# Weighting of one token group moved between engine slots, and two residual adds moved from VectorE to GpSimd, at the end of a recurrent layer with a routed MLP

## The reference, cut to what matters

```python
x2  = layernorm(x)
s   = sigmoid(x2 @ gate_w.T)                       # 32 experts
ids = top_k(s + e_bias, 4); w = s[ids] / sum(s[ids])
y   = sum over the 4 chosen experts of w * ((silu(x2 @ w1[e]) * (x2 @ w3[e])) @ w2[e])
out = x + layernorm(y)
```

## Time and profile before

| | us |
|---|---|
| median of three runs | 341.08 |
| the three runs | 341.17, 339.55, 341.08 |
| the profiled execution, whole | 339.52 |
| its span, first to last instruction | 337.7 |
| busy in the span: PE, DVE, POOL, ACT | 272.0, 250.5, 235.1, 215.6 |
| mean granted TensorE clock | 0.894 of full |

### The profile page before, as it was taken

How to read it: one execution, slowest core, us unless ns; L and a number is a source line. 1 busy time by engine, 2 the same in 40 slices (tenths; PEclk the granted TensorE clock), 3 DMA queues, 4 the chain that set the end, 5 groups by cost and what they waited for, 6 DMA issues and landing times.

```text
span 337.7 us, 6535 instructions
## 1 busy us (share of the span) xinstructions
PE 272.0 (81%) x1489; PEld 218.4 (65%) x1490; DVE 250.5 (74%) x952; ACT 215.6 (64%) x562; POOL 235.1 (70%) x273
## 2 busy tenths in 40 slices
PE   4664586654763989999999999998999999899930
PEld 2243253433642879889887889997967667799810
DVE  3778787887797487697446979863567897698796
ACT  6928867989633545556554556655458858875782
POOL 4396777776777777777763777777777777777700
PEclk9976767978555899999999999999999999999965
DMA  4999999961113455677745899977532111251232
GB/s 103 320 304 287 280 279 287 314 164 48 56 47 94 136 176 175 184 206 208 211 139 161 204 260 267 260 211 211 140 90 54 48 50 51 56 149 47 57 93 63
DMA packets 83999, 54.81 MB, mean 162 GB/s; under 512 B 8032, under 2 KB 80512, under 8 KB 83968
## 3 DMA queue, kind: packets, MB, share of 16 engines
q1 hardware_dynamic: 57472, 30.85, 33.6%
q0 software_dynamic: 6912, 14.17, 14.9%
q10 hardware_dynamic: 19584, 9.44, 9.9%
HBM read 25.07 MB, written 29.36 MB: 161 GB/s over the span
## 4 chain that ended last, share of the span: by engine, by line
PE 61%; DVE 14%; ACT 10%; issue 6%; POOL 6%; DMA 2%; SPq 0%; ACTq 0%; DVEq 0%
PE bank L1758 13%; PE bank L1794 9%; PE bank L1838 6%; PE bank L1826 6%; POOL xs_dram L438 6%; PE bank L1829 5%; PE bank L1775 5%; PE bank L1753 5%; PE bank L1587 4%; PE bank L1628 1%; PE bank L1580 1%; ACT hn L484 1%; ACT xnT L556 1%; DMA wi_raw<-in_L_attn_Wi_dram 1%; DVE left L825 1%
## 5 line engine op out<-in xcount | busy, mean ns | idle before, releaser
L438 POOL DMA_INDIRECT xs_dram<-xn_all,row_xs x108 | 108.3, 1002 | 37.0 <-issue 32.3
L447 POOL DMA_INDIRECT yk<-ys_dram,row_ys x108 | 106.0, 982 | 38.8 <-issue 26.9
L1758 PE MATMUL bank<-w,xbT 128*128 x288 | 59.8, 331 | 0.0
L693 ACT COPY xbT<-bank 128x256 f32<-128x256 f32 x72 | 26.9, 373 | 30.6 <-PE bank L1753 28.8
L1794 PE MATMUL bank<-w2s,aT 96*128 x288 | 45.8, 281 | 0.1
L1758 PEld LDWEIGHTS bank<-w,xbT 128*128 128x128 f32 x288 | 45.6, 192 | 0.2
L1203 DVE TENSOR_TENSOR act_a<-silu,bank 128x192 f32<-128x192 f32 x72 | 25.3, 351 | 26.4 <-ACT silu L696 25.9
L1794 PEld LDWEIGHTS bank<-w2s,aT 96*128 96x128 f32 x288 | 37.7, 191 | 2.0 <-issue 1.3
L696 ACT ACTIVATE silu<-bank 128x192 f32<-128x192 f32 x72 | 23.8, 331 | 18.9 <-PE bank L1758 17.2
L1212 DVE COPY yb<-bank 128x256 f32<-128x256 f32 x72 | 30.3, 421 | 7.3 <-PE bank L1794 5.5
L1838 PE MATMUL bank<-at_at,xn_all 128*128 128x256 f32 (+1 forms) x88 | 31.2, 437 | 3.7 <-DVE at_at L1472 3.7
(11 more groups left out here) (234 smaller groups left out, 526.9 us busy)
## 6 DMA issues: line engine op xcount, KB each, us to landing
xb<-xs_dram SPq DMA_DIRECT2D x144, 64.0 KB
ys_dram<-yb ACTq DMA_DIRECT2D x72, 128.0 KB
xs_dram<-zeros SPq DMA_DIRECT2D x2, 2048.0 KB, 15.0
ys_dram<-zeros SPq DMA_DIRECT2D x1, 2816.0 KB, 13.5
ys_dram<-zeros SPq DMA_DIRECT2D x1, 2560.0 KB, 18.1
x_sb<-in_L_attn_x_dram SPq DMA_DIRECT2D x8, 256.0 KB, 5.4
xs_dram<-xn_all,row_xs POOLq DMA_INDIRECT x108, 4.4
yk<-ys_dram,row_ys POOLq DMA_INDIRECT x108, 2.5
```

Source lines behind the costliest of these rows:

```text
L438: pool.indirect_dma_start(out=xs[h], out_offset=bass.IndirectOffsetOnAxis(ap=row_xs[:, j, k:k + 1], axis=0), in_=xn2_all[:, j, :], in_offs ...
L447: pool.indirect_dma_start(out=yk[h][:, j - h * TP, k, :], out_offset=None, in_=ys[h], in_offset=bass.IndirectOffsetOnAxis(ap=row_ys[:, j, ...
L1758: ins = pe.matmul(ps_gu[o][:, b * 2 * I:(b + 1) * 2 * I].rearrange("t (w a i) -> t w a i", w=2, a=1), xbT[:, o, b, :], w13[:, :, bass.ds(e ...
```

## The change

Five edits, in ACT's, DVE's, POOL's and SP's programs:

1. ACT weights its two tiles of group 6 behind the silus of pieces 41 and 42 instead of behind the loop, and the roots for groups 4 and 5 and the first dense tiles go from behind piece 42 to behind piece 43.
2. DVE does the first three steps of `weigh_in_6` behind piece 43 and the fourth behind piece 45 (before: one behind each of 45, 46 and 47, and the fourth behind the loop).
3. DVE does both `inverse_last` behind piece 44, `norm_d(0)` behind 46, `add_d(0)` behind 47, and the first sum over group 6's ACT-weighted rows also behind 47.
4. The adds of groups 4 and 5 leave DVE; POOL does them behind its last gather, each as one TENSOR_TENSOR of 128x512, waiting for the normed rows (`a_last`) and counting `p_xn`.
5. SP's waits follow: for groups 4 and 5 on `p_xn`, for the rest on a `c_fin` that doesn't count these two.

```diff
+        BY_POOL = [4, 5]
...
             for n, g in enumerate(ORDER):
-                sp.wait_ge(c_fin, n + 1)
+                if g in BY_POOL:
+                    sp.wait_ge(p_xn, 6 + BY_POOL.index(g))
+                else:
+                    sp.wait_ge(c_fin, sum(m not in BY_POOL for m in ORDER[:n + 1]))
...
+            for g in BY_POOL:
+                at = slice(g * GT, g * GT + routed(g))
+                pool.wait_ge(a_last, g + 1)
+                pool.tensor_tensor(x_sb[:, at, :], gathered(g)[:, :, 0, :], x_sb[:, at, :], ALU.add).then_inc(p_xn, 1)
...
-                if e == 42:
+                if e in (41, 42):
+                    weighted(6, e - 41)
+                if e == 43:
                     root_last(1)
                     root_last(2)
...
             act.preload_act_table(ACT.Sqrt)
-            for j in range(by_act(6)):
-                weighted(6, j)
             turned_back(1)
...
                 if e == 43:
+                    weigh_in_6(0)
+                    weigh_in_6(1)
+                    weigh_in_6(2)
+                if e == 44:
                     inverse_last(1)
-                if e == 44:
                     inverse_last(2)
+                if e == 45:
+                    weigh_in_6(3)
+                if e == 46:
                     norm_d(0)
-                if e == 45:
+                if e == 47:
                     add_d(0)
-                if 45 <= e < 48:
-                    weigh_in_6(e - 45)
+                    two_sums(6, by_act(6))
...
-            weigh_in_6(3)
-            add_last(4)
-            add_last(5)
-            two_sums(6, by_act(6))
```

## The result

| | before | change |
|---|---|---|
| median of 13 runs, us | 341.08 | 343.05 |
| lowest and highest, us | 339.55 to 342.24 | 341.99 to 345.39 |
| the profiled execution, whole, us | 339.52 | 343.05 |
| its span, us | 337.7 | 341.3 |

The change over before is 1.0075, with a 95% interval of 1.0053 to 1.0097: slower by 2.0 us in the medians and 2.6 in the ratio, where I forecast 0.3 us less and called that no difference. Timed again, with 12 runs, it was 342.39 against 340.77, 1.0041 (1.0003 to 1.0079). A ratio is formed from the runs themselves, less those in the chip's slower state (here two of the 12), and not from the medians. So it is slower both times; whether by the same amount the intervals don't tell. The traces show two causes, one of which isn't there in every execution.

The account below looks back on a forecast made before the run. From 317 us DVE's program was taken to set the end. A 0.4 us gain less 0.1 for POOL contention made -0.3 us, so 340.8 against the median of 341.08, read as no difference; range 338.6 to 342.5.

Parts of the forecast that it names:

- The order of ACT and of DVE: Table pair between silus of pieces 43 and 44; DVE's three steps, then gaps of about one us before 44 and 45.
- the tail: From the start of group 6's sums on DVE to the end: as before, 9.1 us long.
- The adds gone from DVE: Adds of groups 4 and 5 leave DVE's path, between 325.02 and 326.23: 1.21 us saved.
- I charge 0.1 us: Slowing of DVE beside POOL's adds: 0.1 us, bounds 0 and a whole POOL add of 3.4.
- the third rival: POOL's add of group 4 holds DVE's fourth weighting at about 322.3: up to 3.3 us lost, 344.0; chance 0.12.
- the adds of 401 ns: Early DVE adds with two SBUF inputs beside POOL work: 276 to 401 ns, slowed by up to 0.12 us, not held.
- so it stands 0.5 us: ACT, from 311.98 after piece 41's silu, waits 0.5 us for group 6's last gather, landing at 312.5.
- The second rival: Group 6's gathers land late, at 314.0, moving everything behind ACT's first tile by 1.5 us: 342.3; chance 0.10.
- -0.4: Gain on DVE up to group 6's sums, starting at 325.83 instead of 326.23, before the charge for POOL.

Follow-up runs that it names:

- e1: The change with the adds of groups 4 and 5 back on DVE, behind group 6's first sum: 342.05 against 340.9, 1.0039.
- e5: The change with each of POOL's two adds written as four of 128x128: 341.92 against 340.77, 1.0041.
- b2: Kernel before, DVE's four group 6 weighting steps behind piece 42, ACT's tiles behind piece 44 and the loop, adds on POOL: 339.78 against 340.77, 0.9942.
- after_again: The changed kernel as it is, timed once more: 342.39 against 340.77, 1.0041.
- change_look3: The changed kernel as it is, in one further execution: 341.38 us.
- e3: The change with DVE's fourth weighting step of group 6 one piece earlier, behind the reciprocals of piece 44: 341.66 against 340.9, 1.0039.
- change_look4: The changed kernel as it is, in another single execution: 345.18 us.
- e2: Kernel before with only the adds of groups 4 and 5 on POOL, no weighting moved: 342.04 against 340.9, 1.0058.
- e4: The change with ACT's eight weightings taking group 5's rows into unused tiles, so no wait for group 6's gathers: 340.95 against 340.9, 1.0027.

## Why the prediction was wrong, by its own steps

- **The order of ACT and of DVE: right.** The table pair fell between pieces 43 and 44, the three steps stood ahead of a gap that ends with the silu of piece 44 (0.93 us; I said 1.1), a second gap stood ahead of piece 45 (0.93; I said about one), and the tail took 9.05 us. The adds gone from DVE were worth 1.21.
- **The step "I charge 0.1 us" failed.** From the start of the fourth step to the next piece it took 1.63 us (325.10 to 326.73) where I had put 0.56: the term is 1.07. Its place and its mechanism stood in the text, as the third rival: the step due at 322.3 beside an add due at 322.2; here they start 2.8 and 2.9 later, 0.03 apart. But I had let one reading speak against it, the adds of 401 ns, beside GpSimd work with a single large input, and I priced the rival by a hold of 3.4 us, so that a hold of 1.3 seemed to count for nothing. POOL's add, which I put between 0.61 and 3.4, took 1.26. The Trainium skill, "SBUF — State Buffer", section "Who interferes with whom", says that a DVE instruction with two SBUF inputs and a GpSimd instruction that reads SBUF shut each other out for a whole instruction; e1, e5 and b2 agree with it (0.61 with POOL idle, 1.09 with POOL's add in pieces, no product with a PSUM input held). The adds of at most 401 ns beside GpSimd instructions of 853 don't agree: there a DVE instruction with both inputs in SBUF wasn't held to the end. So what failed is the step from one GpSimd operation to another; why the two differ stays open.
- **The step "so it stands 0.5 us" failed in the other kind of execution.** I took the gather's place from the profile of before and its landing from its own row, and got 0.5 us; three executions of the change's loop (after_again, change_look3, e3) show 0.53, 0.59 and 0.55. What I didn't see is that the place of the gather against the loop has a second value, one gather later; the first profile of the change has it, with 1.99, and so has change_look4 with 2.05. The second rival had the price right (+1.5) but not the cause: no gather landed late, 2.7 us is within; one more gather stood ahead of it.

Put together with the measured terms: -0.4 + 1.07 = +0.7 us with the gather in its early place (seen +0.60 and +0.69), and 1.46 more, +2.1, in its late place (seen +2.05 and +2.14). Against the median of 341.08 that is 341.8 and 343.2: the hold alone would have left the time inside the range, and hold and late place together take it out. The timed ratios of the change, 1.0075 and 1.0041 (2.6 and 1.4 us), have intervals of 1.8 to 3.3 and 0.1 to 2.7 us: the first takes in the late place, the second either. How often each occurs, and what sets the start of the gathers against the loop, wasn't measured: the four traces of the change have two of each, and of all thirteen five have the late place.

## What to carry to other kernels

An instruction moved to an idle engine isn't free when that engine and the one it leaves can hold each other up, as GpSimd and DVE do here: look up what the neighbour runs at that time, and place the moved work beside instructions that read PSUM, as in b2. The trace of before showed the sharing from the other side: a gather that takes 1.49 us among others of 0.94 is one that was held, and such an outlier wants a reason before a term rests on its neighbourhood. Before a wait is put on a stream that runs freely against the loop, count which of its instructions releases it, and ask for the price if the stream is one instruction late.

## What was not expected of the hardware

- The hold works in both directions, and by who starts first only in part. A gather was held in full when it started 0.15 us after DVE's sum, and not when it started up to 0.03 after it. But DVE's fourth step, recorded as starting 0.03 us ahead of POOL's add, was the one that waited (1.70), and so were e2's dense add, 0.18 us ahead (1.88), and the second instruction of e4's fourth step, recorded at 321.88, 0.53 us ahead (1.97). In e2 and e4 POOL's last gather was still under way at that moment. Which event decides isn't visible in the records; this stays open.
- One GpSimd add of 128x512 took 1.26 us, twice DVE's time, and four of 128x128 took 1.80 and 1.69.
- A stream of back-to-back gathers that is held now and then by a regular loop locks to it: over thirteen executions, with starts anywhere from 62.42 to 63.58 us ahead of a fixed instruction, its last gather stood at one of two places, each within 0.04 us.
